# The first norm's inverse deviations repeated over the partitions by DMA through a scratch row, in place of four matmuls, with a new order of the turn

## What is computed

```
h = tok(x) joined with txt                      # (64, 193, 128)
h = h + attn(layernorm(h))
h = h + ffn(layernorm(h))

layernorm(x) = (x - mean(x)) / sqrt(var(x) + 1e-5)      # over the 128 channels
attn: qkv = group_norm(x @ W_qkv); 8 heads;
      logits = q.k + q.rpe_k + k.rpe_q; softmax; attn.v + attn.rpe_v; group_norm
ffn:  8 experts' gelu(w_in @ W1 + b1) @ W2, all of them, once for each of the two
      gate weights of a token (w_in = x * top_p)
```

## Time and profile before

| | us |
|---|---|
| median of three runs | 3127.1 |
| lowest, highest | 3126.92, 3129.14 |
| the profiled execution | 3129.62 |
| its span, first to last instruction | 3127.8 |

### The profile page before, as it was taken

One profiled execution on the slowest core, in us unless ns is written; L12 is line 12 of the kernel. 1 busy time (PEld: TensorE's weight loads), 2 busy tenths in 40 slices (PEclk: granted clock), 3 DMA queues, 4 the chain that ended last, 5 costly groups with the idle time before them and its releaser, 6 DMA issues.

```text
span 3127.8 us, 61794 instructions
## 1 busy us (share of the span) xinstructions
PE 3039.8 (97%) x19776; PEld 2518.8 (81%) x19776; DVE 1897.3 (61%) x4142; ACT 1880.2 (60%) x4370; POOL 1442.8 (46%) x1350
## 2 busy tenths in 40 slices
PE   6997999999999999999999999999999999999998
PEld 5876788888888888888888888888888888888886
DVE  4544566665666666656666666666666666566664
ACT  4642466656655666665655666656656665655567
POOL 1001255554444455554444555544444555444447
PEclk9997899999999999999999999999999999999999
DMA  9971111111100111111101111111001111111010
GB/s 204 220 211 31 27 29 29 29 27 26 28 19 15 29 29 29 27 28 26 29 5 29 29 29 27 28 26 29 14 20 29 29 29 27 27 26 25 6 27 6
DMA packets 92173, 121.58 MB, mean 39 GB/s; under 512 B 8414, under 2 KB 86558, under 8 KB 87710
## 3 DMA queue, kind: packets, MB, share of 16 engines
q1 hardware_dynamic: 87714, 118.24, 16.3%
q10 hardware_dynamic: 4432, 2.99, 0.4%
HBM read 106.23 MB, written 14.97 MB: 39 GB/s over the span
## 4 chain that ended last, share of the span: by engine, by line
PE 86%; ACT 3%; DVE 2%; issue 1%; DMA 0%; POOL 0%; ACTq 0%; POOLq 0%; SPq 0%; DVEq 0%
PE bank L417 19%; PE bank L517 9%; PE bank L518 8%; PE bank L426 7%; PE bank L562 6%; PE bank L563 6%; PE bank L530 6%; PE bank L430 5%; PE bank L427 5%; PE bank L544 3%; PE bank L462 3%; PE bank L572 2%; PE bank L452 1%; PE bank L446 1%; DVE gelu L603 1%
## 5 line engine op out<-in xcount | busy, mean ns | idle before, releaser
L897 POOL TENSOR_TENSOR gelu<-gelu 128x386 f32<-128x386 f32 x1024 | 1055.3, 1049 | 286.9 <-ACT gelu L824 278.2
L823 ACT ACTIVATE gelu<-bank,b_s 128x386 f32<-128x386 f32 x1024 | 596.2, 582 | 626.7 <-DVE gelu L603 600.0
L417 PE MATMUL bank<-gelu,w_s 128*128 128x386 f32 x2048 | 823.7, 489 | 0.3 <-POOL gelu L897 0.3
L603 DVE TENSOR_TENSOR gelu<-bank,ratio 128x386 f32<-128x386 f32 x1024 | 568.0, 557 | 304.5 <-PE bank L430 298.8
L824 ACT ACTIVATE gelu<-gelu,b_s 128x386 f32<-128x386 f32 x1024 | 626.7, 612 | 0.0
L426 PE MATMUL bank<-x_hi,w_hi 128*128 128x386 f32 x1024 | 562.6, 549 | 15.4 <-ACT gelu L823 6.5
L865 ACT ACTIVATE lp<-bank,mx 128x193 f32<-128x193 f32 x800 | 327.9, 420 | 179.2 <-DVE mx L709 176.1
L517 PE MATMUL bank<-k_f,q_bd 128*128 128x193 f32 x1600 | 401.0, 333 | 8.6 <-DVE a_bd L699 8.3
L518 PE MATMUL bank<-rw,a_bd 128*128 128x193 f32 x1600 | 393.7, 328 | 0.0
L417 PEld LDWEIGHTS bank<-gelu,w_s 128*128 128x128 f32 x2048 | 371.3, 189 | 22.4 <-POOL gelu L897 1.2
L910 POOL TENSOR_TENSOR gst<-gst,half 128x4 f32<-128x4 f32 x32 | 32.6, 1017 | 703.9 <-DVE gst L691 703.9
(11 more groups left out here) (132 smaller groups left out, 4528.3 us busy)
## 6 DMA issues: line engine op xcount, KB each, us to landing
a_rep<-u_scratch SPq DMA_DIRECT2D x32, 1600.0 KB, 9.8
xt<-in_x SPq DMA_DIRECT2D x192, 196.0 KB
txt_s<-in_txt SPq DMA_DIRECT2D x32, 128.0 KB, 2.1
u_scratch<-k_f SPq DMA_DIRECT2D x32, 100.0 KB, 2.2
u_scratch<-q_f SPq DMA_DIRECT2D x32, 100.0 KB, 2.2
out<-o_s SPq DMA_DIRECT2D x64, 48.5 KB
out<-o_s SPq DMA_DIRECT2D x64, 48.0 KB
rv<-in_rel_v SPq DMA_DIRECT2D x1, 2624.0 KB, 14.6
```

The lines of the kernel that those rows point to most:

```text
L417: mm(yb[:, 0:T2], w2_s[:, f, :], gelu1[:, f % RING, :], start=(f == 0), stop=(f == NF - 1)).then_inc(S["w2_done"], 1)
L603: v.tensor_tensor(gelu2[:, f % RING, :], zb[f % 2][:, 0:T2], ratio[:, :], ALU.mult).then_inc(S["z2_done"], 1)
L823: a(gelu1[:, f % RING, :], zb[f % 2][:, 0:T2], ACT.Gelu, bias=b1_s[:, f:f + 1]).then_inc(S["g_done"], 1)
L897: g.tensor_tensor(gelu1[:, f % RING, :], gelu1[:, f % RING, :], gelu2[:, f % RING, :], ALU.add).then_inc(S["hs_done"], 1)
```

## The change

`bc1` leaves TensorE. SyncE, at the head of `spread(t)`, now waits for `rs1` (`rstd1`), writes its four columns into a DRAM row `r_scratch` with four DMAs, waits until all four have landed, and reads the row back with one DMA that repeats it over 128 partitions into a new SBUF tile `r_bc`. DVE multiplies by that tile in `bc1`. And `SCHEDULE` is another one. Of its long line the moved words are these (before, then after):

```diff
-... c c am0 vt hkeep qs0 qs1 c qs2 c qs3 log0 am1 qs4 log1 log2 txt am2 log3 log4 am3 log5 ...
+... c c qs0 qs1 am0 vt c hkeep c log0 am1 log1 qs2 am2 qs3 log2 log3 txt log4 log5 am3 ...
-... log12 tr0 c bc1 inv tr1 rel0 c tr2 rel1 tr3 rel2 tr4 rel3 tr5 rel4 tr6 rel5 rel6 c proj pv0 ...
+... log12 tr0 c tr1 c rel0 tr2 rel1 tr3 c inv rel2 tr4 rel3 tr5 bc1 rel4 tr6 rel5 rel6 proj c pv0 ...
-... nqk c c oaff c c onorm c oh2 c c mean2 c c var2 top c gate c c gate2 nv c c bcast ...
+... nqk c c oaff c onorm c c oh2 c mean2 c c var2 nv top c gate c c gate2 c c bcast ...
```

```diff
+        r_bc = sb("r_bc", [P, T2])
...
+            def repeat_rstd(t):
+
+                sp.wait_ge(S["rstd1"], t + 1)
+                for k, (a, b) in enumerate(zip(GO, GO[1:] + [T2])):
+                    sp.dma_start(r_scratch[a:b].unsqueeze(1), rs1[0:b - a, k:k + 1]).then_inc(S["r_out"], 16)
+                sp.wait_ge(S["r_out"], t * 64 + 64)
+                sp.dma_start(r_bc[:, :], r_scratch[0:T2].unsqueeze(0).broadcast_to([P, T2])).then_inc(S["rstd_bc1"], 16)
+
             def spread(t):
+                repeat_rstd(t)
...
-                elif s == "bc1":
-                    pe.wait_ge(S["rstd1"], t + 1)
-                    broadcast(misc, rs1).then_inc(S["rstd_bc1"], 1)
...
-                    dve.wait_ge(S["rstd_bc" + k], t + 1)
-                    v.tensor_tensor(V2(sq), V2(delta), ps[:, 0:T2], ALU.mult).then_inc(S["x" + k], 1)
+                    dve.wait_ge(S["rstd_bc" + k], t * 16 + 16)
+                    v.tensor_tensor(V2(sq), V2(delta), r_bc[:, :], ALU.mult).then_inc(S["x" + k], 1)
```

More of the change, by code:

```diff
@@ L84 @@
 SCHEDULE = (
-    "c c am0 vt hkeep qs0 qs1 c qs2 c qs3 log0 am1 qs4 log1 log2 txt am2 log3 log4 am3 log5 log6 log7 log8 log9 log10 mean1 log11 var1 log12 tr0 c bc1 inv tr1 rel0 c tr2 rel1 tr3 rel2 tr4 rel3 tr5 rel4 tr6 rel5 rel6 c proj pv0 gmean rec0 pv1 rec1 gvar place0 c place1 c omean c gaff ovar c c c c c nqk c c oaff c c onorm c oh2 c c mean2 c c var2 top c gate c c gate2 nv c c bcast w2t w2t xin w2t a w2t ot a a otr hres ocopy"
+    "c c qs0 qs1 am0 vt c hkeep c log0 am1 log1 qs2 am2 qs3 log2 log3 txt log4 log5 am3 log6 log7 log8 qs4 log9 log10 mean1 log11 var1 log12 tr0 c tr1 c rel0 tr2 rel1 tr3 c inv rel2 tr4 rel3 tr5 bc1 rel4 tr6 rel5 rel6 proj c pv0 gmean rec0 pv1 rec1 gvar place0 c place1 c omean c gaff ovar c c c c c nqk c c oaff c onorm c c oh2 c mean2 c c var2 nv top c gate c c gate2 c c bcast w2t w2t w2t xin a w2t ot a a otr hres ocopy"
 ).split()
@@ L249, in _, with fused_block @@
                         nc.vector.tensor_copy(xs[0:ROWS, slot, s:s + QS0, :], steps(slot, s, s + QS0)).then_inc(dve_packed, 1)
-def fused_block(nc, txt, w1, tok_scratch, u_scratch, out, R):
+def fused_block(nc, txt, w1, tok_scratch, u_scratch, r_scratch, out, R):
     with ExitStack() as ctx:
@@ L312, in fused_block @@
         names = """w1_in w1_hi_ready w1_split setup_dve setup_pool setup_act tok_in txt_t h_ready qk_ready v_ready
-            bn mv_ready gmean gspread gvar gve grstd affine_part affine norm q_spread a_spread a_masked u_out log_ready max_done log_done
+            bn mv_ready gmean gspread gvar gve grstd affine_part affine norm q_spread a_spread a_masked u_out r_out log_ready max_done log_done
             vt v_copied tr_ready tr0_copied tr1_copied wm_done pv_done pv_ready inv_part inv_ready rec_done o_part obn omv omean ospread ovar ove orstd oaff_part oaffine
@@ L941, in build @@
     u_scratch = nc.dram_tensor("u_scratch", (2, DK, BH, LP), F32, kind="Internal").ap()
+    r_scratch = nc.dram_tensor("r_scratch", (T2 + 2,), F32, kind="Internal").ap()
     with ExitStack() as ctx:
@@ L944, in build @@
         patch_embed(nc, a, tok_scratch, R)
-        fused_block(nc, a["txt"], a["w1"], tok_scratch, u_scratch, out.rearrange("b l c -> (b l) c"), R)
+        fused_block(nc, a["txt"], a["w1"], tok_scratch, u_scratch, r_scratch, out.rearrange("b l c -> (b l) c"), R)
 def shape_constants(np):
```

## The result

| | before | with the change |
|---|---|---|
| median (us) | 3127.1 | 3143.0 |
| lowest, highest of 7 | 3124.8, 3129.7 | 3135.7, 3148.6 |
| profiled span | 3127.8 | 3142.7 |
| steady turn | 88.79 | 88.10 to 88.15 when nothing is late |

The ratio is 1.0047, with a 95% interval of 1.0035 to 1.0060. The kernel became slower by 15.9 us; 28 us less was forecast.

The account below looks back on a forecast made before the run. TensorE, busy 97% of the span, was taken to bound the kernel. Removing `bc1` (-27.0), moving `am2` (-8.7) and the start (+7.8) sum to -27.9, so 3127.1 becomes 3099 us; range 3089 to 3113.

Parts of the forecast that it names:

- 1.0 for the semaphore and the issue of the read: SyncE, between the landing of the four column writes and the read into `r_bc`: 1.0 us.
- the 9.9 us of the latency: DMA chain from `rs1` to `r_bc`: 6.3 for the writes, 1.0 for semaphore and issue, 2.6 for the read.
- the 6.3 for them: The four column writes to DRAM: 6.3 us, taken from stores with as many rows, 97 rows running on one engine.
- the high bound: DMA chain at its longest: two 6.7 us columns in series on one engine and 3.6 for the rest, 17.0 us.
- The read: The DMA of 193 KB into `r_bc`: 2.6 us, from 2.1 for 128 KB and a little more.
- the cover of 17.2: In a steady turn the tile may come as late as 17.2 us after SyncE begins without TensorE waiting at `rel6`.
- rival A: DVE at `bc1`, then TensorE at `rel6`: DMA latency x exceeds its cover, kernel slower, 3164 at x = 19; 8%.
- The start: Pair 0 has nothing beside it, so the DMA chain stands on the path: +7.8 us, between +3.6 and +14.9.
- The first turn: This turn has no feed-forward pieces, so the cover is 13.7 us, still enough for 9.9.
- The moved pieces: Feed-forward pieces, `nv` and `onorm` moved in the turn: no difference, bound 0.3 us a turn either way, 9 us in all.
- rival B: TensorE regains its 0.87 only in part, waiting at `tr1`, `rel0` or `onorm`: 0.5 us a turn lost, 3114; 13%.
- `bc1` gave its 0.87 a turn and `am2` its 0.29: `bc1` off TensorE: 0.87 us a turn, 27.0 in all; `am2` earlier in the logits: 0.29 a turn, 8.7 in all.

Follow-up runs that it names:

- Base: The changed kernel itself, as the follow-up runs start from it: 3143.0 us, ratio 1.0047 against the kernel before.
- experiment 5: Base with each column write cut to 96 rows and the two elements left over written by a DMA each: 3119.3 us, ratio 0.9965.
- experiment 9: As experiment 3, plus four writes of 96 rows of 4 bytes, elements 64 bytes apart, to a DRAM tile nobody reads: 3114.8 us, ratio 0.9957.
- experiment 3: Base with the four column writes replaced by one write of 128 rows of 16 bytes, read back whole: 3114.9 us, ratio 0.9953.
- experiment 6: As experiment 3, but the one 16-byte-row write has 97 rows in place of 128: 3114.6 us, ratio 0.9949.
- experiment 4: Base with ScalarE's `nv` back ahead of `bcast`: 3145.0 us, ratio 1.0053.
- experiment 8: As experiment 3, with the feed-forward piece behind `tr3` moved back ahead of `mean2`: 3114.1 us, ratio 0.9950.
- experiment 1: The kernel before with only the new `SCHEDULE`, `bc1` still on TensorE: 3136.6 us, ratio 1.0029.
- experiment 2: Base with the `SCHEDULE` of before, so the DMAs with the old order: 3608.1 us, ratio 1.1533.
- experiment 7: As experiment 3, with a feed-forward piece between `var2 nv` and `top` instead of behind `top`: 3103.7 us, ratio 0.9914.

## Why the prediction was wrong

**The step that failed: "1.0 for the semaphore and the issue of the read", in the 9.9 us of the latency.** Windows of the turn shown above, with the packets of the writes (and of the text tokens ahead of them), and from there to the read:

```profile
1531.00:1536.20 5.20, 5.20 (x39) 4.61 (x38) 2.25 (x5) 4.29 (x7) 3.26 (x4) 1.00 0.21 26
1536.20:1542.80 6.60, 6.60 (x56) 6.33 (x55) 3.82 (x8) 2.28 (x4) 0.20 (x1) 1.00 0.00 0
```

The packets of the writes end at about 1536.2, 5.6 us after the first issue, so the 6.3 for them was near. While they last, two or three of the sixteen engines are busy (share 0.1 to 0.2). Behind them come 6.6 us in which no DMA engine shows a packet (share 0.00), and only then is the read issued. That is the term which the prediction had at 1.0. In windows of 0.2 us over the pairs of Base (but for the one in the first turn, where the share does not fall to nothing until later) the packets end 4.8 to 6.4 us after the first issue, and the stretch behind them lasts 4.2 to 8.7. In experiment 5, with 96 rows in each DMA, the packets end sooner, after 2.6 as a rule, and the empty stretch is still 6.1 to 8.3. In experiment 9, where the elements stand 64 bytes apart, it is 0.2 to 1.1, and with 16 bytes a row (experiments 3 and 6) 0.2 to 1.4. So the empty stretch is the price of neighbouring 4-byte elements, with or without columns of 97 rows; these columns add some 3 us of packets (5.6 against 2.6).

The Trainium skill says in "DMA: Bandwidth & Descriptors", specifications, that below 512 B a transfer is a read-modify-write. The runs show that smallness alone is not what costs, since 16-byte elements land in 1.9 us (experiment 3) and spaced 4-byte elements in 1.5 us a DMA (experiment 9). Reads and writes of the same few bytes that wait for one another would explain why neighbours are slow, but that is argued, not shown. I had one row for 4-byte elements, the 6.7 us of `vec`. It is a load, and I used it as the high bound only, against the nearer-looking stores.

**The read: 4.7, not 2.6.** I scaled a DMA that spreads 128 KB by its bytes. All 128 copies of `r_bc` come from one 1.5 KB row. The 256 KB of experiment 3, from a 2 KB row, took 3.5, and 3.1 in experiment 9, so bytes don't order these. Why 193 KB take longer than 256 stays open.

**The high bound: 17.0, "covered, barely".** The real range of 14.3 to 19.6 passes both it and the cover of 17.2. That is rival A, which had 8%. Its mechanism was right down to the place, DVE at `bc1` and TensorE at `rel6`. Its form was not: I had reckoned with one x for all turns, and the latency differs by 5 us from turn to turn, so ten turns were late and cost 14.0, where x = 19 in each would have cost 56. With each turn's own x (its distance and 4.7 for the read) the rival's term x - 17.2 adds up to 14.9, so its size was right too. Of the 14.0 the waits at `rel6` show 9.8 (13.4 less the 3.6 of the first turn). Part of the rest is the clock in the turn that is 3.8 late: from 1191.40 to 1211.40 TensorE works 18.08 of 20 us at a granted clock of 0.91; in the same stretch of the other late turns it is 1.00. The remainder was not followed.

**The start: +14.7, not +7.8.** Here nothing covers the chain, and the term takes the whole error of the latency: 11.45 for the writes from the last issue on, and 4.41 for the read. The bound of +14.9 held, narrowly. In experiment 3 this is +3.6, the same as the low bound.

**The first turn: +6.0, not 0.** From the first write at 298.86 to the tile at 317.26 there are 18.4 us, 4.7 more than the cover of 13.7. TensorE waited 3.65 for it, so the cover was about 1 us longer than reckoned. A second cost came with it that I had not counted. Two windows that follow one another there:

```profile
312.00:318.00 6.00, 3.06 (x28) 2.87 (x26) 0.71 (x2) 0.27 (x1) 0.00 (x0) 0.93 0.45 33
318.00:330.00 12.00, 10.81 (x118) 6.54 (x118) 5.51 (x25) 0.00 (x0) 1.01 (x1) 0.75 0.01 1
```

TensorE worked 3.06 of the 6 us up to 318, and after that its granted clock is 0.75 for 12 us: 0.50 (1.2 GHz) up to 324 and 1.00 (2.4 GHz) from there. The eight matmuls of the q and k projections, 0.81 before, take 1.49 there, and TensorE's work from the end of the wait to the end of its last matmul ahead of DVE (L579) takes 10.13 (318.70 to 328.83), where it took 7.42 before (300.69 to 308.11). With these 2.7 and the wait of 3.65 it is 6.4, for the 6.0 measured. This wait of TensorE cost more than its length.

**The moved pieces: "I take no difference, with 0.3 us a turn either way as bound", and 0.55 was lost.** The edits that I weighed near this place were `nv` and `onorm`. What got late was DVE. Timelines of DVE, GpSimd, ScalarE and TensorE at `top` in a turn of the change:

```profile
1670.02 1.14 DVE L769 TENSOR_TENSOR dl<-top 97x4 f32<-97x4 f32 x1
1670.12 1.01 POOL L904 TENSOR_TENSOR gelu<-gelu 128x386 f32<-128x386 f32 x1
...
1671.08 0.55 DVE L610 TENSOR_TENSOR gelu<-bank,ratio 128x386 f32<-128x386 f32 x1
...
1671.66 0.58 ACT L830 ACTIVATE gelu<-bank,b_s 128x386 f32<-128x386 f32 x1 [0.47 <-DVE gelu L610]
...
1672.30 0.44 PE L436 MATMUL bank<-x_hi,w_hi 128*128 128x386 f32 x1 [0.29 <-ACT gelu L830]
```

The reader is to see a chain of four engines. The small subtraction ends together with GpSimd's addition, 0.9 us late; the scaling of the next piece starts behind it; ScalarE's gelu waits 0.47 for that, and TensorE waits for the gelu, which frees its bank. Pieces follow each other at 1.73 there where 1.18 is usual. Before, the same subtraction took 0.23, in the same kernel text, beside the same addition:

```profile
L762 DVE TENSOR_TENSOR dl<-top x32: 167/232/233, 320.7 to 3068.5; 97x4 f32<-97x4 f32 x32
```

The Trainium skill has the rule in "SBUF — State Buffer", section on who interferes with whom: a DVE instruction with both inputs in SBUF contends with a GpSimd instruction that reads SBUF, the contention is an exclusive lock, and the order of issue decides who blocks. The trace agrees in the length: 1.14 against the addition's 1.01. It doesn't settle the order: by the records the subtraction starts 0.10 ahead of the addition in the change, and 0.11 ahead before, where it isn't held up. What tips it in the new order stays open: not `nv` (experiment 4), not the place of `mean2` (experiment 8), not the DMAs (it is in experiment 1, and gone in experiment 2 with the old order, where it takes 0.23). The other moves were not tried one by one; the new `SCHEDULE` also has `qs4` behind `log8` and a third `w2t` ahead of `xin`, which the lines of the change do not show. That the loss goes through it is borne out by experiment 7: the long subtraction is gone, TensorE's waits for a gelu there (L435 in that kernel) fall from 16.0 to 6.8 us against experiment 3, and the turn wins 0.37 of the 0.55 a turn. The other 0.18 stands elsewhere. There TensorE waits in each turn for GpSimd's addition, at the product with W2 (L426 in that kernel): 8.6 us in 33 places, where the kernel before had 1.2 us in two. Engine, line and what was waited for in experiment 7; us in total, times, longest:

```profile
PEld bank L426 <- POOL gelu L906: 8.6, 33, 0.9
```

The 0.55 us a turn is what rival B said in size (0.5 us a turn) and not in mechanism: it looked at ScalarE's copies and `onorm`.

**What was right.** `bc1` gave its 0.87 a turn and `am2` its 0.29: a steady turn is shorter by 0.65, and 0.87 + 0.29 - 0.55 is within 0.04 of it. By experiments 1 and 3 the removal gave 0.90 a turn (89.03 to 88.13). The logits show no step above 0.33 but one of 0.44, which stood there before as well. The order alone in experiment 1 should give -0.29 + 0.55 = +0.26 a turn, and 0.24 was measured; experiment 3 gives from there -27.0 + 3.8 at the start, 3111.6 for a span of 3112.2. SyncE was never late for `k_f`, and the cover of 17.2 held: turns with a sum below it were not late.

## What to carry to other kernels

Write a column of small elements to DRAM so that each row of the DMA carries several of them; four neighbouring columns of 4 bytes cost 10 to 15 us where the same numbers in 16-byte rows cost 1.4 to 3. Elements that stand 64 bytes apart land fast too, but reading them back was not tried. The time of a DMA's packets is not the time to its semaphore, so look at both. A latency that is to be hidden wants a margin for its spread, since the cover of 17.2 us was passed by some turns and not by others, and a stretch without cover, such as a pipeline's first turn, is worth a path of its own. Before a small DVE operation is moved, look which GpSimd instruction stands beside it.

## What the runs showed of the hardware that was not expected

- 386 neighbouring 4-byte elements in DRAM: 8.7 to 10.9 us from the first issue to the read that waits for all of them when no DMA has 97 rows (experiment 5), 9.6 to 14.9 with two that do. Through 6.8 of these us (6.6 in the turn shown of Base) no DMA engine shows a packet. 384 such elements 64 bytes apart, beside a write of 2 KB: 3.3 to 4.2 (experiment 9).
- One DRAM row read back over 128 partitions: 193 KB in 4.7 us as 386 elements, 194 KB in 3.7 as 388, 256 KB in 3.1 to 3.5 as 512. The first two differ by two elements and by how the row had been written; which of them counts was not tried.
- A 97x4 subtraction on DVE takes 0.17 alone and 1.14 beside a GpSimd addition, though its record starts 0.10 ahead of the addition's.
